# A conv kernel with routed experts: lots of patches, four images side by side, and a table of expert pairs loaded ready made

## The reference, cut to what matters

```
feat = patched.mean(axis=(2, 3));  logits = feat @ Wg + bg
routing = one_hot(argmax(logits), 8) * softmax(logits)
y_e = relu(conv3x3(patched, Wexp[e]) + bexp[e])
out = x + unpatchify(sum_e routing[:, e] * y_e)[:, :, :32, :32]
```

## Time and profile before

| | |
|---|---|
| median of 3 runs | 221.12 us (217.77 to 224.03) |
| the profiled execution | 215.9 us |
| its span in the trace | 213.8 us |
| PE / DVE / ACT / POOL busy | 53% / 65% / 38% / 37% |
| moved by DMA | 44.91 MB, 210 GB/s over the span |

### The profile page before, as it was taken

The page is one execution under the profiler, slowest core; times in us unless marked ns, Lnnn a source line. Parts: engine busy times, 40 slices in busy tenths (PEclk is TensorE's granted clock), DMA queues, the critical chain, the costliest instruction groups (busy, mean ns, idle before and its releaser), DMA issues.

```text
span 213.8 us, 11088 instructions
## 1 busy us (share of the span) xinstructions
PE 113.7 (53%) x4880; PEld 104.7 (49%) x4880; DVE 139.9 (65%) x273; ACT 81.7 (38%) x242; POOL 79.1 (37%) x207
## 2 busy tenths in 40 slices
PE   0000308666179637476559746745767759466620
PEld 0000308656179527365458646635656658455620
DVE  3889793336992589564995699367946990383145
ACT  2391349009600591019502940096006900650000
POOL 8489429109400580019201920094006800670000
PEclk9999999889956996789575896799585875988995
DMA  6868997962499577996499478987499869902002
GB/s 225 325 269 200 272 342 179 240 167 96 168 288 246 172 304 173 242 265 223 168 289 264 137 295 209 239 235 249 157 286 261 317 154 229 285 22 101 6 3 98
DMA packets 82415, 44.91 MB, mean 210 GB/s; under 512 B 77888, under 2 KB 78016, under 8 KB 81344
## 3 DMA queue, kind: packets, MB, share of 16 engines
q1 hardware_dynamic: 81792, 43.21, 72.0%
q10 hardware_dynamic: 576, 1.00, 1.3%
HBM read 29.77 MB, written 14.43 MB: 207 GB/s over the span
## 4 chain that ended last, share of the span: by engine, by line
PE 44%; issue 24%; DVE 17%; ACT 5%; ACTq 4%; DMA 2%; POOLq 2%; POOL 0%; DVEq 0%
PE conv_bank L395 38%; DVE SUMS L216 5%; ACT WIND L325 4%; ACTq L101 3%; PE pick_bank L383 3%; DVE NEWT L202 2%; DVE PROD L221 2%; DMA XT<-x 2%; PE logit_bank L374 2%; DVE XN L210 2%; POOLq L101 2%; DVE GATE L223 1%; DVE BLK L263 1%; PE pick_bank L385 1%; DVE BLK L268 1%
## 5 line engine op out<-in xcount | busy, mean ns | idle before, releaser
L395 PE MATMUL conv_bank<-XG,WS 128*32 128x64 f32 x4800 | 103.3, 256 | 62.3 <-issue 56.4
L395 PEld LDWEIGHTS conv_bank<-XG,WS 128*32 128x32 f32 x4800 | 94.2, 134 | 69.0 <-issue 68.8
L165 POOL COPY WS<-WP 128x192 f32 x200 | 60.1, 353 | 107.1 <-issue 93.5
L335 ACT COPY WS<-WP 128x192 f32 x200 | 52.1, 348 | 51.3 <-issue 43.7
L257 DVE STREAM_TRANSPOSE YT<-conv_bank 128x320 f32<-128x320 f32 x40 | 19.1, 499 | 16.6 <-PE conv_bank L395 16.6
L216 DVE TENSOR_REDUCE SUMS<-WIND 128x25 f32<-128x2500 f32 x8 | 22.1, 2759 | 10.9 <-ACT WIND L325 10.8
L245 DVE TENSOR_SCALAR IDX<-pick_bank 1x57 int32<-1x57 f32 x8 | 1.7, 206 | 29.3 <-PE pick_bank L385 29.3
L374 PE MATMUL logit_bank<-GATE,CONST 128*100 128x8 f32 x32 | 5.4, 278 | 26.8 <-DVE GATE L223 26.8
L325 ACT COPY WIND<-XN 128x2500 f32<-128x2500 f32 x8 | 18.8, 2350 | 1.7 <-DVE XN L210 1.7
L374 PEld LDWEIGHTS logit_bank<-GATE,CONST 128*100 128x100 f32 x32 | 4.7, 221 | 27.8 <-issue 21.9
L263 DVE STREAM_TRANSPOSE BLK<-YT 128x1024 f32<-128x1024 f32 x8 | 16.8, 2100 | 0.1
(11 more groups left out here) (28 smaller groups left out, 54.3 us busy)
## 6 DMA issues: line engine op xcount, KB each, us to landing
XG<-windows SPq DMA_DIRECT2D x24, 1000.0 KB, 10.1
windows<-WIND SPq DMA_DIRECT2D x8, 1250.0 KB, 5.1
XT<-x SPq DMA_DIRECT2D x8, 512.0 KB, 4.4
out<-XT SPq DMA_DIRECT2D x16, 256.0 KB, 4.5
CONST<-consts ACTq DMA_DIRECT2D x1, 390.0 KB, 4.6
BLK<-wtab ACTq DMA_DIRECT2D x1, 384.0 KB, 9.5
WGS<-wgs ACTq DMA_DIRECT2D x1, 200.0 KB, 6.2
BG<-bg ACTq DMA_DIRECT2D x1, 4.0 KB, 8.1
```

Source lines behind the costliest of these rows:

```text
L165: last = nc.gpsimd.tensor_copy(WS[:, at % RING, ACT_PAIRS + i, :], WP[:, bass.ds(index[lot * POOL_PAIRS + i], PAIR)])
L335: last = nc.scalar.copy(WS[:, at % RING, i, :], WP[:, bass.ds(index[lot * ACT_PAIRS + i], PAIR)])
L395: last = nc.tensor.matmul(o, WS[:, at % RING, n % LOT * 2 + b // 2, column:column + C], taps, start=kx == 0, stop=kx == TAPS - 1)
```

## The change

**The table of pairs.** The host lays out all 64 pairs; `wtab` is now 97 rows of 12288 floats, 4.77 MB, and one request on ACT's queue brings it into `WP`. The two copies, the two memsets and the buffer `WT` are gone. All tiles of the convolution now have `KP` = 97 partitions: 96 for (channel, vertical tap), one for the bias, whose row of ones comes by a request of its own (`ones`).

**Patches side by side.** The rows of the windows in DRAM now hold one window of each of the four images (`SPAN` = 400 floats). A write is four requests, one for each image, in runs of 400 bytes; a read of a lot is three requests of 32x5 runs of 1520 bytes (`READ` = 380 floats).

**The ring.** `XG` is a ring of `RX` = 8 lots; each lot is read, waited for and freed by itself. The first group's windows are written in pieces: the first `FIRST` = 7 channels of each image in four requests on SP's queue, the other 25 channels in two requests on SP's queue and two on ACT's. `XT` has five buffers instead of four.

**The order.** `normalise` moves from DVE to ACT. The window sums are taken from `XN` in two steps. POOL spreads the probabilities (`spread`, over 16 places instead of 128). Indices are read into registers lot by lot. The logits of group g+2 are made after lot 3 of group g, and before the loop those of group 1; the last lot of a group is transposed in the next pass.

The core of the diff (not shown: new semaphores, constants, `routing` cut in two, moved waits):

```diff
-KROWS = PS * WIN
-ROWS = TAPS + 1
+KP = TAPS * C + 1
...
+RX = 8
+FIRST = -(-LOT * C // NP)
+SPAN = GI * WIN * WIN
+READ = SPAN - WIN * WIN + PS * WIN
...
-        XG = [sb(f"XG{u}", [128, GN, KROWS]) for u in range(2)]
-        WS = sb("WS", [128, RING, PAIRS, PAIR])
-        WP = sb("WP", [128, E * E * PAIR])
+        XG = sb("XG", [KP, RX * LOT, SPAN])
+        WS = sb("WS", [KP, RING, PAIRS, PAIR])
+        WP = sb("WP", [KP, E * E * PAIR])
...
             def write_windows(g):
-                u = g % 2
                 sp.wait_ge(windows_ready, g + 1)
                 if g > 1:
-                    sp.wait_ge(taps_loaded[u], 16 * TAPS * (g // 2))
-                sp.dma_start(windows_dram[u].rearrange("(p k) w -> p (k w)", k=NP), WIND[:]
-                             ).then_inc(windows_written, 16)
-
-            def read_patches(g):
-                u = g % 2
-                sp.wait_ge(windows_written, 16 * (g + 1))
-                if g > 1:
-                    sp.wait_ge(conv_done, LOTS * (g - 1))
+                    for at in range((g - 2) * LOTS, (g - 1) * LOTS):
+                        sp.wait_ge(taps_loaded[at % RX], 16 * TAPS * (at // RX + 1))
+                for b in range(GI):
+                    sp.dma_start(window_rows(g % 2, b, 0, C), window_tile(b, 0, C)).then_inc(windows_written, 16)
+
+            def load_taps(g, lot):
+                at = g * LOTS + lot
+                source = windows_dram[g % 2].rearrange("(n j) w -> j n w", j=C)[:, lot * LOT:(lot + 1) * LOT]
                 for ky in range(TAPS):
-                    rows = bass.AP(XG[u], ky * GN * KROWS, [[ROWS * GN * KROWS, C], [KROWS, GN], [1, KROWS]])
-                    sp.dma_start(rows, windows_dram[u].rearrange("(n j) w -> j n w", j=C)
-                                 [:, :, ky * WIN:ky * WIN + KROWS]).then_inc(taps_loaded[u], 16)
+                    rows = bass.AP(XG, (ky * RX + at % RX) * LOT * SPAN,
+                                   [[TAPS * RX * LOT * SPAN, C], [SPAN, LOT], [1, READ]])
+                    sp.dma_start(rows, source[:, :, ky * WIN:ky * WIN + READ]).then_inc(taps_loaded[at % RX], 16)
+
+            def read_lot(g, lot):
+                at = g * LOTS + lot
+                sp.wait_ge(windows_written, 16 * GI * (g + 1))
+                if at >= RX:
+                    sp.wait_ge(conv_done, at - RX + 1)
+                load_taps(g, lot)
...
-            for g in range(XB):
+            for g in range(4):
                 load_x(g)
-            write_windows(0)
-            sp.wait_ge(ones_set, 1)
-            read_patches(0)
+            sp.wait_ge(windows_ready, 1)
+            for b in range(GI):
+                sp.dma_start(window_rows(0, b, 0, FIRST), window_tile(b, 0, FIRST)).then_inc(first_written, 16)
+            for b in range(GI // 2):
+                sp.dma_start(window_rows(0, b, FIRST, C), window_tile(b, FIRST, C)).then_inc(windows_written, 16)
+            sp.wait_ge(first_written, 16 * GI)
+            load_taps(0, 0)
+            for lot in range(1, LOTS):
+                read_lot(0, lot)
             write_windows(1)
-            sp.wait_ge(ones_set, 2)
+            read_lot(1, 0)
+            read_lot(1, 1)
             for g in range(GROUPS):
                 if g + 1 < GROUPS:
-                    read_patches(g + 1)
+                    read_lot(g + 1, 2)
+                if g > 0 and g + 3 < GROUPS:
+                    if g + 3 >= XB:
+                        sp.wait_ge(out_stored, 32 * (g + 3 - XB + 1))
+                    load_x(g + 3)
+                if g + 2 < GROUPS:
+                    write_windows(g + 2)
+                if g + 1 < GROUPS:
+                    read_lot(g + 1, 3)
                 if g > 0:
                     stores(g - 1)
-                if g > 0 and g + XB - 1 < GROUPS:
-                    sp.wait_ge(out_stored, 32 * g)
-                    load_x(g + XB - 1)
-                if g + 2 < GROUPS:
-                    write_windows(g + 2)
+                if g + 1 < GROUPS:
+                    read_lot(g + 1, 4)
+                if g + 2 < GROUPS:
+                    read_lot(g + 2, 0)
+                    read_lot(g + 2, 1)
             stores(GROUPS - 1)
...
-            nc.gpsimd.memset(XG[0][:], 1.0).then_inc(ones_set, 1)
+            def spread(g):
+                pool.wait_ge(own_ready, g + 1)
+                if g > 0:
+                    pool.wait_ge(spread_ready, g)
+                if g > 2:
+                    pool.wait_ge(out_ready, 2 * (g - 2))
+                span = [CONST[:, C_SPAN + SPREAD * i:C_SPAN + SPREAD * (i + 1)] for i in range(2)]
+                nc.gpsimd.tensor_scalar(PARTS[:, 0:SPREAD], span[0], PTWO[g % 2][:, 0:1], None, ALU.mult)
+                nc.gpsimd.tensor_scalar(PARTS[:, SPREAD:], span[1], PTWO[g % 2][:, 1:2], None, ALU.mult
+                                        ).then_inc(pool_chain, 1)
+                pool.wait_ge(pool_chain, g + 1)
+                nc.gpsimd.tensor_tensor(PBM[g % 3][:], PARTS[:, 0:SPREAD], PARTS[:, SPREAD:], ALU.add
+                                        ).then_inc(spread_ready, 1)
...
             pool.wait_ge(table_loaded, 16)
-            nc.gpsimd.tensor_copy(bass.AP(WP, 0, [[E * E * PAIR, 128], [E * PAIR, E], [PAIR, E], [1, NW]]),
-                                  bass.AP(BLK, 0, [[H * W, 128], [NW, E], [0, E], [1, NW]])).then_inc(pairs_laid, 1)
-            nc.gpsimd.memset(XG[1][:], 1.0).then_inc(ones_set, 1)
-            pool.wait_ge(pairs_laid, 2)
             for g in range(GROUPS):
                 pool.wait_ge(index_ready, g + 1)
-                index = pick_rows(pool, g, POOL_AT, LOTS * POOL_PAIRS)
                 for lot in range(LOTS):
-                    copies(g, lot, index)
+                    copies(g, lot)
+                    if lot == 1:
+                        spread(g)
...
+                nc.vector.scalar_tensor_tensor(NEGMR[:], MV[:, 0:1], -1.0, RSTD[:], ALU.mult, ALU.mult
+                                               ).then_inc(rstd_ready, 1)
 
             def gate(g):
-                dve.wait_ge(windows_ready, g + 1)
-                nc.vector.tensor_reduce(SUMS[:], WIND[:].rearrange("p (k w) -> p k w", k=NP),
-                                        AX.X, ALU.add).then_inc(sums_ready, 1)
+                dve.wait_ge(normalised, g + 1)
+                nc.vector.tensor_reduce(
+                    bass.AP(ROWSUM, 0, [[NB * PITCH, 128], [PITCH, KEEP], [1, W + 2]]),
+                    bass.AP(XN, 0, [[PITCH * PITCH, 128], [PS * PITCH, KEEP], [1, W + 2], [PITCH, WIN]]),
+                    AX.X, ALU.add)
+                then_next(nc.vector.tensor_copy(ROWSUM[:, KEEP * PITCH:KEEP * PITCH + W + 2],
+                                                XN[:, H * PITCH:H * PITCH + W + 2]))
+                nc.vector.tensor_reduce(
+                    SUMS[:].rearrange("p (v h) -> p v h", v=NB),
+                    bass.AP(ROWSUM, 0, [[NB * PITCH, 128], [PITCH, NB], [PS, NB], [1, WIN]]),
+                    AX.X, ALU.add).then_inc(sums_ready, 1)
...
+                dve.wait_ge(spread_ready, g + 1)
+                patches = BLK[:].rearrange("p (k w) -> p k w", w=PIX)
+                prob = bass.AP(PBM[g % 3], 0, [[SPREAD, 128], [1, SPREAD], [0, PIX]])
+                then_next(nc.vector.scalar_tensor_tensor(patches, patches, 0.0, prob, ALU.max, ALU.mult))
                 for v in range(KEEP):
-                    prob = bass.AP(PBM[g % 3], v * W, [[KEEP * W, 128], [0, PS], [1, W]])
-                    strip = BLK[:, v * PS * W:(v + 1) * PS * W].rearrange("p (i h) -> p i h", i=PS)
-                    last = nc.vector.scalar_tensor_tensor(strip, strip, 0.0, prob, ALU.max, ALU.mult)
-                then_next(last)
-                for q in range(2):
-                    rows = XT[g % XB][:, q * HALF:(q + 1) * HALF]
-                    nc.vector.tensor_tensor(rows, BLK[:, q * HALF:(q + 1) * HALF], rows, ALU.add).then_inc(out_ready, 1)
-
-            nc.vector.memset(XN[:], 0.0).then_inc(pads_set, 1)
+                    rows = XT[g % XB][:, v * PS * W:(v + 1) * PS * W].rearrange("p (i h w) -> p h i w", i=PS, h=KEEP)
+                    strip = BLK[:, v * PS * W:(v + 1) * PS * W].rearrange("p (h i w) -> p h i w", i=PS, h=KEEP)
+                    last = nc.vector.tensor_tensor(rows, strip, rows, ALU.add)
+                    if v % 2 == 1:
+                        last.then_inc(out_ready, 1)
...
+            def normalise(g):
+                act.wait_ge(rstd_ready, g + 1)
+                if g > 0:
+                    act.wait_ge(windows_ready, g)
+                    act.wait_ge(sums_ready, g)
+                inside = bass.AP(XN, PITCH + 1, [[PITCH * PITCH, 128], [PITCH, H], [1, W]])
+                nc.scalar.activation(inside, XT[g % XB][:].rearrange("p (h w) -> p h w", w=W), ACT.Identity,
+                                     bias=NEGMR[:], scale=RSTD[:]).then_inc(normalised, 1)
...
+            def copies(g, lot):
```

(96 more changed lines are left out.)

92 lines of the change are left out of this document (42 added, 50 removed).

## The result

The changed kernel takes 421.44 us (median of 4 runs, 420.42 to 423.07) against 219.59 us for the kernel before on the same chip: ratio 1.935, 95% interval 1.927 to 1.943. The forecast was 387 us with a range of 351 to 428.

A forecast was written before the change was run, and what follows sets the result against it. Waits, mostly on PE, were taken to bound the kernel; after the change, 198 (table landing) + 10 + 1 (to first matmul) + 166 (PE's stretch) + 7.9 (tail) = 383 us, plus 2.1 around and 2 for the median: 387, range 351 to 428.

The forecast's parts named there:

- The table on one engine: Kernel start: 97 rows dealt to one DMA engine, 181 to 186 us, landing taken at 198 us; mechanism's chance 0.80.
- the other of the two cases that I had named: Start: window traffic on the table's engine stands back, is paid afterwards; table lands at 188 to 190 us, not 202.
- ACT held by its own queue: Start: ACT possibly held issuing window requests behind the table; exponent(0) and indices then come a few us after landing.
- From landing to the first matmul: Between table landing and convolution: copies, normalise, sums and logits(1) take 10 us, plus 1 us for lot 1.
- PE's stretch: From the convolution's first matmul until the tail: 166 us, between 155 and 179, from 173.3 before.
- off the chain: PE's stretch: tap reads (8.9 us a group) and window writes (4.7 us at worst) run ahead, so PE doesn't wait.
- the high end: Upper range: one engine at 22.8 GB/s, landing at 227, stretch 175, tail 9; 428 us with the median's surplus.
- The reading of "issue" as program fetch: PE's stretch: pauses of 1.3 to 2 us after every 128 matmuls are PE waiting for its next piece of program.
- The sums on DVE: Window sums, before the gate and in each group: 1.8 us instead of 2.76, as fewer elements are read.
- normalise on ACT: Moved from DVE to ACT, after the first copies and in each group: 1.1 us.
- The rival: Start: table dealt over all 16 engines, landing at about 21 us; 209 us in all, faster by 5%; chance 0.13.
- The tail: After PE's stretch: the same last transposes, scaling and store, 7.9 us, give or take 1.

The follow-up runs named there:

- e6: e5_first_whole with 128 rows again, four per channel and three used, table in one request, ones set by POOL: 231.9 us, ratio 1.060.
- e11: The kernel before with 97 rows instead of 128 in the convolution's tiles, its 384 KB table in requests of 96 rows and 1 row: 241.3 us, ratio 1.110.
- e7: e5_first_whole without the window writes to DRAM for groups 2 to 7: 241.1 us, one run.
- e8: e7 with taps read for the first eight lots only, later lots reusing them: 213.1 us, one run.
- e1: The changed kernel with the table's request cut in two, 96 rows and 1 row: 264.8 us, ratio 1.221.
- e5_first_whole: e1 with the first group's windows written like all others, four requests of 32 channels on SP's queue: 261.1 us, ratio 1.198.

## Why the prediction was right, and where it was off

**The table on one engine** was right, mechanism and price: 3.4 + 184 and some sharing were to land it at 198 us. No wait in the trace gives its landing, but ACT came free at 187.3 and copied out of it from 190.8. The traffic of the windows stood back instead of squeezing in, the other of the two cases that I had named. The rule of the Trainium skill for the engine count ("DMA: Bandwidth & Descriptors", "Why a DMA increments its semaphore by 16 and not by 1") is borne out by 97, 96, 112 and 102 rows. By the 27 GiB/s for one engine in its "Specifications" the table would take an estimated 164 us; it took about 184, as the 26 GB/s of the trace had it. What I named as possible, ACT held by its own queue, is in the trace for 175 us, and seems to have cost little, since PE could not start anyhow.

**From landing to the first matmul**: 10 + 1 us expected, 17 found (187.3 to 204.5). That the first matmul came at 204.5 where 198 + 10 + 1 = 209 was forecast is two errors that nearly cancel. Of the 17 us, 3.4 are exponent(0) and the indices, which come only after ACT is free; 10.0 are the chain as added up, from the first copy at 190.8 to the end of logits(1) at 200.8; and 3.7 are a wait that the profile does not name, most likely for lot 0, whose reads are issued from 189.8 us on and land 9.2 us after issue.

**PE's stretch was mis-sized**, and this is the term behind nearly the whole error of the total: 166 us, with a bound of 179, against 207.4. I took the reads as helped by runs of 1520 bytes at 411 GB/s (8.9 us a group) and the writes in runs of 400 bytes as nearly cancelling. Two things failed there. I gave a rate that rows four apart had reached to rows three apart, and said only of matmuls that 97 rows change nothing; e6 and e11 put 16 and 24 us of stretch on that, all of it in slower matmuls. And I said that transfers are off the chain, because PE never waited for taps. It doesn't, and yet its stretch grows with the traffic: longer pauses (73.5 instead of 56.4 us), a granted clock of 0.50 over 220 to 300 us, and matmuls of 285 instead of 256 ns. e7 and e8 show that PE's stretch shortens as traffic is taken away, though PE waits for none of it. How much of the slower clock follows from the pauses was not separated; in e11 the clock is lower (0.63 over the stretch, before 0.81) with pauses no longer than before.

**The range held by luck of its width.** With the first matmul at 204.5, the upper bound of 179 for the stretch, the tail and what surrounds the span, about 395 us could come out at most. That 421 lies within 351 to 428 is owed to 29 us that the high end held for a slower DMA engine (landing at 227), which did not come. The high end also used 175 for the stretch, less than the bound named.

**The reading of "issue" as program fetch** stands: e8 rules out taps and weights, and the 38 packets of 16 KB fit the count; it remains a reading. **The sums on DVE** were put at 1.8 us and took 3.2 (2.59 for the first step, over columns 42 apart, against 2.76 for the whole before); harmless, as DVE is not the bound. **normalise on ACT** took 1.27, not 1.1. **The rival** of an even deal of 97 rows did not happen; its time of 209 us would not have been reached even with sixteen engines, as e1 shows: 265 us. **The tail** was right: 8.1 us from the start of the last matmul to the end.

## What to carry to other kernels

Count the rows of a large request before its bytes: 97 rows went over one DMA engine, and 96 and 1 in their place gave back 157 us. Price the spacing of the partitions that a request writes, too: rows three apart came in more slowly than rows four apart, and packing 128 rows into 97 cost 11% by itself. Give added traffic a price in PE's own time, even where PE waits for none of it in the trace: here the writes lengthened its pauses and the reads its matmuls.

## What I had not expected of the hardware

- At the same busy share of the DMA engines, a request for 96 rows of 49 KB moved 202 GB/s, one for 128 rows 426 GB/s.
- Reads into 32 rows three apart moved 192 GB/s, into 32 rows four apart 274 GB/s, runs of 320 bytes both.
- An engine that issues a request behind a busy one in its queue can be held in that issue itself, here ACT for 175 us.
- A small DVE copy stood still for 11.1 us beside POOL's copy and memset, and 4.6 us with the memset gone.
- The granted clock in the rows can fail to show slow matmuls. In e5_first_whole it reads 1.00 from 50 to 110 us, while the median matmul there takes 313 ns, as it does at 0.50 (130 to 160 us); at a true 1.00 it takes 218 (before, 70 to 77 us):

```profile
80.00:90.00 10.00, 8.29 (x253) 7.62 (x246) 4.38 (x9) 6.15 (x16) 3.85 (x13) 1.00 1.01 237
```
